# Two-relation graph layer: the low parts of the edge counts applied through a few selected rows

## The reference, cut to what matters

```python
w = jnp.einsum('rb,bio->rio', att, basis)
x_j = x[col]
for r in range(NUM_RELATIONS):
    gate = jax.nn.sigmoid(x_j @ gate_w[r, :, 0])
    msgs.append(gate[:, None] * x_j @ w[r])
msg = jnp.where((edge_type == 0)[:, None], msgs[0], msgs[1])
agg = jax.ops.segment_sum(msg, row, num_segments=x.shape[0])
return agg + x @ root + bias
```

## Time and profile before

| | |
|---|---|
| runs (three) | 842.68 us median, 841.76 to 845.55 |
| the profiled execution | 841.44 us, its span 839.4 us |
| TensorE (PE) busy | 811.3 us, 97% |
| TensorE weight loads (PEld) | 618.9 us, 74% |
| VectorE (DVE) | 555.1 us, 66% |
| ScalarE (ACT) | 397.6 us, 47% |
| GpSimd (POOL) | 279.4 us, 33% |
| DMA | 115.78 MB, 138 GB/s |

### The profile page before, as it was taken

The page is one execution under the profiler, slowest core; times in us unless marked ns, Lnnn a source line. Parts: engine busy times, 40 slices in busy tenths (PEclk is TensorE's granted clock), DMA queues, the critical chain, the costliest instruction groups (busy, mean ns, idle before and its releaser), DMA issues.

```text
span 839.4 us, 13163 instructions
## 1 busy us (share of the span) xinstructions
PE 811.3 (97%) x4174; PEld 618.9 (74%) x4175; DVE 555.1 (66%) x1223; ACT 397.6 (47%) x646; POOL 279.4 (33%) x296
## 2 busy tenths in 40 slices
PE   5999989999899999999999999999999999999998
PEld 3665646677578778778687787887777967688786
DVE  7999998787878677477656665683767666720210
ACT  5999985345455523366323465134562344530300
POOL 5000015434442235702366222556112725542200
PEclk9999999999999999999999999999999999999999
DMA  7899956727416544763473736547435786020100
GB/s 190 171 238 231 280 144 168 179 81 196 134 51 140 167 102 135 176 156 114 94 201 101 178 80 190 117 141 167 104 124 154 187 223 175 26 101 0 51 13 38
DMA packets 60655, 115.78 MB, mean 138 GB/s; under 512 B 4520, under 2 KB 5104, under 8 KB 60596
## 3 DMA queue, kind: packets, MB, share of 16 engines
q1 hardware_dynamic: 43412, 81.33, 40.2%
q10 hardware_dynamic: 17184, 33.69, 12.2%
HBM read 107.67 MB, written 7.34 MB: 137 GB/s over the span
## 4 chain that ended last, share of the span: by engine, by line
PE 67%; DVE 5%; ACT 1%; issue 1%; DVEq 0%
PE ring L2098 26%; PE ring L1788 19%; PE ring L2405 5%; PE ring L1806 5%; PE mix_ps L1817 4%; PE ring L2392 3%; PE ring L2333 1%; PE ring L2334 1%; DVE stats L1207 1%; PE ring L2287 1%; PE ring L2288 1%; PE ring L2292 1%; DVE xl L1585 1%; PE ring L2364 1%; DVE yp L1523 1%
## 5 line engine op out<-in xcount | busy, mean ns | idle before, releaser
L703 POOL TENSOR_TENSOR wl<-wraw,wh 128x512 fp32r<-128x512 f32 x140 | 181.1, 1324 | 265.2 <-ACT wh L809 253.7
L712 POOL TENSOR_TENSOR rstd<-ve,half 128x1 f32<-128x1 f32 x48 | 26.9, 561 | 209.0 <-DVE ve L1212 208.7
L1890 PE MATMUL ring<-ohs,ohd 128*128 128x512 f32 x312 | 80.0, 407 | 4.3 <-DVE ohs L1385 4.2
L1890 PEld LDWEIGHTS ring<-ohs,ohd 128*128 128x128 f32 x312 | 58.3, 193 | 30.1 <-issue 17.1
L1363 DVE SCALAR_TENSOR_TENSOR ohd<-iota,dstT,vals 128x256 fp32r x156 | 69.0, 477 | 3.4 <-issue 2.4
L809 ACT ACTIVATE wh<-wraw 128x2048 fp32r<-128x2048 f32 x35 | 66.8, 1909 | 5.2 <-PE ring L1788 4.9
L834 ACT ACTIVATE yT_h<-ring 128x512 fp32r<-128x512 f32 x32 | 18.4, 598 | 97.9 <-PE ring L1806 97.9
L858 ACT ACTIVATE ohs<-iota,minus_srcT 128x512 fp32r<-128x512 f32 x78 | 52.7, 714 | 8.7 <-issue 6.4
L1194 DVE TENSOR_TENSOR PT_l<-ring,PT_h 128x512 fp32r<-128x512 f32 x64 | 39.6, 681 | 16.0 <-ACT PT_h L834 16.0
L1817 PE MATMUL mix_ps<-quad,att_shift 120*32 120x512 f32 x384 | 46.8, 599 | 0.0
L834 ACT ACTIVATE qk_h<-ring,bias_columns 128x512 fp32r<-128x512 f32 x32 | 22.1, 690 | 51.8 <-PE ring L1788 43.7
(11 more groups left out here) (390 smaller groups left out, 2146.5 us busy)
## 6 DMA issues: line engine op xcount, KB each, us to landing
quad<-in_L_gnn_basis SPq DMA_DIRECT2D x60, 960.0 KB, 10.6
wraw<-in_L_gnn_m_w ACTq DMA_DIRECT2D x8, 1024.0 KB, 6.5
mix_scratch<-mixed SPq DMA_DIRECT2D x128, 32.0 KB
wraw<-in_L_gnn_wv ACTq DMA_DIRECT2D x4, 1024.0 KB, 8.1
wraw<-in_L_gnn_wq ACTq DMA_DIRECT2D x4, 1024.0 KB, 5.5
wraw<-in_L_gnn_wk ACTq DMA_DIRECT2D x4, 1024.0 KB, 5.3
wraw<-in_L_gnn_wo ACTq DMA_DIRECT2D x4, 1024.0 KB, 6.7
wraw<-mix_scratch ACTq DMA_DIRECT2D x4, 1024.0 KB, 5.7
```

What stands on the lines that cost most here:

```text
L703: last = g.tensor_tensor(wl[s][:, k, :], wraw[s][:, k, :], wh[s][:, k, :].bitcast(F32), ALU.subtract)
L1890: last = te.matmul(ring[:, banks[b], :], ohd[:, s, b, :], ohs[:, s, :], start=False, stop=False)
```

## The change

All of it is in the last stage.

- **Counts.** The matmuls with `C_l` are left out of `R(l, m)`: two matmuls for each relation and row tile in place of three. A count below 4096 has no low part, and among 16384 edges at most four counts can reach it, so at most four rows of each tile need one. VectorE finds in `far_flags` (after the first relation's four Z tiles) the largest count of each row, clears a selector `far_sel` of 8 x 128 columns and marks the rows at or above 4096. A product with a triangle of ones, the tile `order`, ranks them; `far_selectors` turns the ranks into selection columns. TensorE then gathers the chosen rows of `C_l` into a tile `far` (8 matmuls, once) and of `Z_h` into `near` (8 matmuls, for each l), both at full width, VectorE copies them to SBUF, and one matmul `near` by `far` goes into each `R(l, m)`. The gathering comes after `R(l, 0)`, and R(l, 0) and R(l, 1) are both closed after the matmuls of R(l, 1).
- **Gates.** `gwh` and `gwl` become one `gw` of four columns; 4 x two matmuls in place of 4 x three. The 4x512 result is copied by ScalarE as it is, four small fp32 products with a 4x2 matrix of ones and zeros (`gate_sum`) transpose it and add high and low parts, and ScalarE takes the exp of the 128x8 result.
- **Elsewhere.** GpSimd makes the triangle and the numbers between two weights' low parts; `far_sel`, `far` and `near` lie where `Cr` was; the small tables lie in `mask`, which is free by then. Three tiles are added to `n3` for l = 0 (`order`, `far`, `near`) and one for l = 1.

```diff
@@ tiles of the last stage @@
-                   + [n for l in range(2) for n in [("g", l)] + [("Z", l, r, t) for r in range(2) for t in range(4)]
-                      + [("R", l, t) for t in range(4)]], n2.end)
+                   + [("g", 0)] + [("Z", 0, 0, t) for t in range(4)] + [("Z", 0, 1, t) for t in range(3)]
+                   + ["order", ("Z", 0, 1, 3), "far", ("near", 0)] + [("R", 0, t) for t in range(4)]
+                   + [("g", 1)] + [("Z", 1, r, t) for r in range(2) for t in range(4)]
+                   + [("near", 1)] + [("R", 1, t) for t in range(4)], n2.end)
@@ GpSimd @@
+            low_weight(W3, slot(W3))
+            g.affine_select(out=far_upto, in_=ones[:], compare_op=ALU.is_ge, fill=0.0, base=0,
+                            pattern=[[1, P]], channel_multiplier=-1).then_inc(far_numbers, 1)
+            g.iota(far_no.rearrange("p (a e) -> p a e", e=STRIP), [[-FAR, 2 * NT], [1, STRIP]], base=1, channel_multiplier=0,
+                   allow_small_or_imprecise_dtypes=True).then_inc(far_numbers, 1)
+            low_weight(W3 + 1, slot(W3 + 1))
@@ ScalarE @@
-                a.activation(gate_e[:], ring[0:2, n3.bank(("g", l)), :], ACT.Exp, scale=-1.0).then_inc(gate_exp, 1)
+                a.activation(gate_raw, ring[0:4, n3.bank(("g", l)), :], ACT.Copy).then_inc(gate_raws, 1)
                 act.drain().then_inc(tile_taken, 1)
+                act.wait_ge(gate_rows, l + 1)
+                a.activation(gate[:], mix_ps[:, 0:2 * NT], ACT.Exp, scale=-1.0).then_inc(gate_exp, 1)
@@ VectorE @@
+            v.tensor_tensor(gate_sum, ident[0:4, 0:2], ident[0:4, 2:4], ALU.add).then_inc(gate_sums, 1)
...
+            def far_flags():
+
+                for r in range(2):
+                    v.reduce_max(far_top[:, r * NT:(r + 1) * NT], f(C_h[:, r, :, :]), AX.X).then_inc(far_step, 1)
+                v.memset(far_sel[:].bitcast(F32), 0.0).then_inc(far_step, 1)
+                dve.wait_ge(far_step, 3)
+                v.tensor_scalar(far_flag, far_top, EXACT, None, ALU.is_ge).then_inc(far_step, 1)
+
+            def far_selectors():
+                ready(n3, n3.base, "order")
+                dve.wait_ge(far_step, 4)
+                v.tensor_tensor(far_rank, bank(n3, "order")[:, 0:2 * NT], far_flag, ALU.mult).then_inc(tile_taken, 1)
+                taken(n3, n3.base, "order")
+                dve.wait_ge(far_numbers, 2)
+                each = lambda ap: ap.unsqueeze(2).broadcast_to([P, 2 * NT, STRIP])
+                v.tensor_tensor(far_eq.rearrange("p (a e) -> p a e", e=STRIP), far_no.rearrange("p (a e) -> p a e", e=STRIP),
+                                each(far_rank), ALU.is_equal).then_inc(far_step, 1)
+                dve.wait_ge(far_step, 5)
+                v.tensor_tensor(far_sel[:, :, 0:STRIP], far_eq.rearrange("p (a e) -> p a e", e=STRIP), each(far_flag), ALU.mult).then_inc(far_step, 1)
@@ VectorE, in the loop over l @@
+                        if l == 0 and r == 1 and t == 2:
+                            far_selectors()
+                    if l == 0 and r == 0:
+                        far_flags()
+                if l == 0:
+                    ready(n3, n3.base, "far")
+                    v.tensor_copy(far[:], bank(n3, "far")).then_inc(tile_taken, 1)
+                ready(n3, n3.base, ("near", l))
+                v.tensor_copy(near[:], bank(n3, ("near", l))).then_inc(tile_taken, 1)
@@ TensorE @@
+            def chosen_rows(name, of):
+
+                multiply(begin(n3, B, name), [(far_sel[:, r * NT + t, :], of[:, r, t, :]) for r in range(2) for t in range(NT)]
+                         ).then_inc(tile_ready, 1)
...
-                    for n, (lhs, rhs) in enumerate(three(gwh[:, l, k, :], gwl[:, l, k, :], h[:, k, :], hl[:, k, :])):
-                        last = te.matmul(out, lhs, rhs, start=k + n == 0, stop=k == KT - 1 and n == 2)
+                    te.matmul(out[0:4, :], gw[:, l, k, :], h[:, k, :], start=k == 0, stop=False)
+                    last = te.matmul(out[0:2, :], gw[:, l, k, 0:2], hl[:, k, :], start=False, stop=k == KT - 1)
...
+                        if l == 0 and r == 1 and t == 2:
+                            pe.wait_ge(far_numbers, 1)
+                            pe.wait_ge(far_step, 4)
+                            te.matmul(begin(n3, B, "order")[:, 0:2 * NT], far_upto, far_flag, start=True, stop=True).then_inc(tile_ready, 1)
                         if r == 0 and t == 2 - l:
-                            pe.wait_ge(gate_exp, l + 1)
+                            pe.wait_ge(gate_raws, l + 1)
+                            pe.wait_ge(gate_sums, 1)
                             pe.wait_ge(set_taken, SETS + 1)
                             for j in range(NT):
-                                last = te.transpose(mix_ps[:, 2 * j:2 * j + 2], gate_e[:, j * P:(j + 1) * P], ident[0:2, 0:2])
+                                last = te.matmul(mix_ps[:, 2 * j:2 * j + 2], gate_raw[:, j * P:(j + 1) * P], gate_sum, start=True, stop=True)
...
-                            if l == 0:
-                                pairs = three(z[:, m * P:(m + 1) * P], zl[:, m * P:(m + 1) * P], C_h[:, r, t, :], C_l[:, r, t, :])
-                            else:
-                                pairs = three(C_h[:, r, t, m * P:(m + 1) * P], C_l[:, r, t, m * P:(m + 1) * P], z, zl)
+                            for part in (z, zl):
+                                if l == 0:
+                                    te.matmul(out, part[:, m * P:(m + 1) * P], C_h[:, r, t, :], start=False, stop=False)
+                                else:
+                                    te.matmul(out, C_h[:, r, t, m * P:(m + 1) * P], part, start=False, stop=False)
+
+                def far_relations(m):
+                    c = slice(m * P, (m + 1) * P)
+                    lhs, rhs = (near[:, c], far[:]) if l == 0 else (far[:, c], near[:])
+                    te.matmul(outs[m], lhs, rhs, start=False, stop=True).then_inc(tile_ready, 1)
+
+                relations(0)
+                if l == 0:
+                    pe.wait_ge(far_step, 6)
+                    pe.wait_ge(c_ready, 2)
+                    chosen_rows("far", C_l)
+                chosen_rows(("near", l), Z_h)
+                relations(1)
+                taken(n3, B, ("near", l))
+                far_relations(0)
+                far_relations(1)
+                for m in range(2, NT):
+                    relations(m)
+                    far_relations(m)
```

More of the change, by code:

```diff
@@ L68 @@
 INTO_L3 = INTO_L2 + NT
+EXACT = 4096.0
+FAR = STRIP // (2 * NT)
+assert EDGES // EXACT <= FAR
 EPS = 1e-5
@@ L196, in program @@
         layer_bias = sb("layer_bias", [P, KT])
-        gate_e = mask[0:2, 0, :]
+        gate_raw = mask[0:4, 0, :]
+        gate_sum = mask[0:4, 2, 0:2]
+        far_upto = mask[:, 1, 0:P]
+        far_no = mask[:, 1, P:3 * P]
+        far_top = mask[:, 1, 3 * P:3 * P + 2 * NT]
+        far_flag = mask[:, 1, 3 * P + 2 * NT:3 * P + 4 * NT]
+        far_rank = mask[:, 1, 3 * P + 4 * NT:3 * P + 6 * NT]
+        far_eq = mask[:, 2, 2 * P:4 * P]
         gate = sb("gate", [P, 2 * NT])
@@ L331, in program @@
         C_l = sb("C_l", [P, 2, NT, NODES], F32R, ctx=c3)
-        Cr = [sb(f"Cr{r}", [P, NT, NODES], I16, ctx=c3) for r in range(2)]
+        counted = ExitStack()
+        Cr = [sb(f"Cr{r}", [P, NT, NODES], I16, ctx=counted) for r in range(2)]
+        counted.close()
+        far_sel = sb("far_sel", [P, 2 * NT, P], F32R, ctx=c3)
+        far = sb("far", [P, NODES], F32R, ctx=c3)
+        near = sb("near", [P, D], F32R, ctx=c3)
         c3.close()
@@ L402, in program @@
         row_bias_loaded = [sem(f"row_bias_loaded{j}") for j in range(2)]
+        gate_raws = sem("gate_raws")
         row_biased = sem("row_biased")
+        gate_sums = sem("gate_sums")
         end_bias_loaded = sem("end_bias_loaded")
@@ L413, in program @@
         c_ready = sem("c_ready")
+        far_numbers = sem("far_numbers")
+        far_step = sem("far_step")
         gate_exp = sem("gate_exp")
@@ L782, in _ @@
             block_lows(BLOCKS - 1, True)
-            for w in (W3, W3 + 1):
-                low_weight(w, slot(w))
+            low_weight(W3, slot(W3))
[4 more added lines that the diff above has]
+            low_weight(W3 + 1, slot(W3 + 1))
             for t in range(NT):
@@ L1291, in selectors @@
                 v.tensor_tensor(sel[:, 0, :], f(sel[:, 0, :]), f(sel[:, 1, :]), ALU.add)
-                v.tensor_copy(gwh[:], gates).then_inc(sel_step, 1)
+                v.tensor_copy(gw[:, :, :, 0:2], gates).then_inc(sel_step, 1)
                 v.tensor_copy(bg[:, :, 0:2], bias).then_inc(sel_step, 1)
@@ L1296, in selectors @@
                 dve.wait_ge(sel_step, 6)
-                v.tensor_tensor(gwl[:], gates, f(gwh[:]), ALU.subtract).then_inc(sel_step, 1)
+                v.tensor_tensor(gw[:, :, :, 2:4], gates, f(gw[:, :, :, 0:2]), ALU.subtract).then_inc(sel_step, 1)
```

(19 more changed lines are left out.)

9 lines of the change are left out of this document (4 added, 5 removed).

## The result

The changed kernel takes 836.43 us in the median of six runs (835.25 to 838.71), the kernel before, beside it on the same chip, 842.47 (six runs, 841.76 to 845.55). The ratio is 0.9923, with a 95% interval of 0.9909 to 0.9937: faster by 0.8%, 6.0 us by the medians. The forecast was 835.6 us, with a range of 833.2 to 838.6. The profiled execution took 836.25 us with a span of 834.4, where 834.3 and 832.3 were forecast.

The account below looks back on a forecast made before the run. TensorE bounds the kernel, busy 811.3 of 839.4 us. Terms -14.51 - 1.85 + 7.25 + 0.29 + 1.0 + 0.75 = -7.1 us give 835.6 us from the median of 842.68, range 833.2 to 838.6.

Parts of the forecast that it names:

- Removed matmuls, gatherings and closings: TensorE, last stage: 64 matmuls with `C_l` removed, -14.51 us; 32 gathering and closing matmuls of the same shape added, +7.25 us.
- The gate matmuls: Gates on TensorE: one matmul in three goes, 4 for each layer, 8 x 0.231 = 1.85 us saved.
- `order`: TensorE's ranking product in full fp32, 128 rows and 8 columns: 0.29 us added, nothing if it slips between two others.
- The small products: Gates: four fp32 products replace four transposes in each layer, 0.5 us more a layer, 1.0 for both (0.7 to 1.6).
- The stall before the second layer's products: TensorE waits 0.66 to 0.92 us, taken as 0.75, for ScalarE's gates' tile reading, held by the root weight's transfer.
- The wait for `hT_l`: Before the last gate matmuls: not new, ending 1.35 us after R(0, 3), covered by six matmuls of 1.39 us.
- The flags' cover: `far_flags` on VectorE is ready before TensorE reaches `order`: hidden, by 0.1 to 0.9 us.
- GpSimd, the copies, the banks: GpSimd's tables fit a 2.46 us gap, copies run under R(l, 1), shifted banks were taken earlier: no cost.
- The bounds: The main forecast's 834.5 to 836.8 us, from the products, the stall and spare time at `order`; chance 0.70.
- late flags: Rival, chance 0.12: VectorE's reductions or clearing are slower, TensorE waits 1 to 3 us at `order`, 836.6 to 838.6 us.
- the costly gathering: Rival, chance 0.05: selections and closings cost over 0.2267 us each, or closing hides a 2 to 3 us wait; 838.8 us.
- The fall of the clock: Rival, chance 0.03: a stall drops TensorE's clock from 2.4 to 1.2 GHz, each matmul losing 0.227 us; slower.

Follow-up runs that it names:

- the kernel with the transposes: Changed kernel, but TensorE transposes the gates' four rows as before and VectorE adds high and low parts: 834.48 us, ratio 0.9892.
- the kernel with the early reading: Changed kernel with gates transposed, VectorE adding the parts, and ScalarE reading the second layer's gates' tile before rounding the root weight: 833.93 us, ratio 0.9888.
- doubled flags: Changed kernel with VectorE computing the two row maxima of the counts twice, so the flags are late: 841.14 us, ratio 0.9973.
- changed again: The changed kernel as it is, measured and profiled once more against the kernel before: 835.9 us, ratio 0.9917.
- gates alone: The kernel before with only the gates' part of the change, the counts as before: 841.96 us, ratio 0.9993.
- later wait: Changed kernel with the row maxima computed twice and `order` moved behind the last Z tile: 837.79 us, ratio 0.9949.

## Why the prediction was right

The sum was -7.1 us and the stage became 7.20 us shorter. By its terms:

- **Removed matmuls, gatherings and closings** (-14.51 and +7.25): right. R of the first layer is 2.73 us shorter, and 12 x 0.2267 = 2.72 remain when 20 matmuls come in for 32. Behind the second layer's products it is 3.83 + 0.71 (the products' own) = 4.54, and 20 fewer are 4.53. The kernel without the gathering confirms 7.25 us by 7.38, of which 0.07 stand before the second layer's products and 0.07 are the products'.
- **The gate matmuls** (-1.85): right as work, 8 in 1.85 us where there were 12 in 2.77.
- **`order`** (+0.29): 0.12 us and 0.13 more for the tile behind it, 0.25.
- **The small products** (+1.0): mis-sized. They took 0.98 and 1.05 us for 0.34 each, +1.35, and the kernel with the transposes gives the same 1.3 back. I put them nearer to the transposes because only four rows are loaded; the larger products of the earlier trace rows, at 0.145 us an instruction, were the nearer end. The load of the stationary operand took 0.12 us for each of eight instructions (0.96 us), and the eight loads of 128 rows for the products of the earlier trace rows took 0.97. The Trainium skill, TensorE: Matmul & The Clock Gate, section LDWEIGHTS (loading the stationary operand), says that the load goes by the operand's columns and not by its rows; the trace agrees for these two. A transpose's load of the same four rows and 128 columns took 0.08 (0.32 us for four); why a product's load is longer, no run here shows. The Trainium skill, FP8 and Floating Point Precision, section TensorE Precision Notes, has true FP32 take four passes through the array. An estimate from that alone made the products of two columns next to free, and the 1.35 us speak against it.
- **The stall before the second layer's products** (+0.75): the mechanism exists, but its size was read from one landing of the transfer, and in the first profile it is all but absent. The products came 7.57 us after R(0, 3), not 7.95 to 8.21. TensorE's work is 7.29 us, so 0.28 us were lost, and 0.20 of that is the wait for `hT_l`: the kernel with the early reading, where ScalarE is not waited for, needs 7.50. At most 0.07 us is left for ScalarE. The idle time of 0.7 to 0.9 us that was to show the stall is not there. From the transfer's issue to the start of the rounding it took 4.95, 4.98 and 5.08 us in three executions with products (no gathering, doubled flags, changed), and they came after 7.50, 7.54 and 7.57; 5.41, 5.41 and 5.46 in three others (changed again, gates alone, later wait), with 7.88, 7.88 and 7.93. The upper end of 8.21 was a misreading: the 0.26 us between ScalarE's end and the weight load in the earlier trace rows were TensorE's own arrival, for where TensorE does wait, the load follows 0.05 us after ScalarE (785.74 to 785.79).
- **The wait for `hT_l`** (nothing, "not new"): it is new. Three matmuls for each value of k put nine ahead of that wait, two put six. `hT_l` was ready at 779.00 and the sixth matmul through at 779.03, as counted (1.35 us against 1.39), but the next weight load stands behind the same wait and began only at 779.05, and that cost 0.20 us.

The errors, +0.35 on the products and -0.47 on stall and wait together, nearly cancel. That the sum fits to 0.1 us is in that part luck. The conclusion drawn from them held all the same: the second layer's gates gave back all that they saved, 8.61 us from R(0, 3) to the end of the products against 8.55 before.

The terms put at nothing, and the bounds:

- **The flags' cover**: ready 0.8 us before TensorE, where 0.1 to 0.9 was argued for. Both reductions took 4.47 us, the clearing 0.91.
- **GpSimd, the copies, the banks** (nothing): as argued.
- **The bounds** 834.5 to 836.8 are wider than what is named for them: 0.3 us less to 0.6 more for the products, 0.09 less to 0.17 more for the stall and 0.29 less for `order` give 834.9 to 836.4.

The forecast of the span was 2.1 us low, though the stage was 0.1 us better than forecast. The step from one profiled span to the other passed over a spread that the profile of one execution can't show: the first 118 us differ by up to 1.7 us between executions of one kernel. The medians, 6.0 and 6.9 us apart in the two measurements, are less open to it.

Of the rivals, late flags and the costly gathering did not occur; the stall was all but gone in the first profile and there, at half its size, in the second. The fall of the clock did not occur in the stage either, but it is real: it came behind a wait of 3.5 us, and those of the change come to less than 0.6 us together in this part of the stage. Had the reductions run at half their rate, the case that I priced at 839 to 840 us, the run with four of them says 841 in the median, and 839 where the clock stayed up: I priced the wait there and not the clock behind it.

## What to carry to other kernels

Where one engine's chain has no gap, count its matmuls times their start-to-start time and look at each place where another engine hands over; the sum came within 0.1 us here, with two errors of 0.35 and 0.47 us that offset each other. A selection made by matmuls costs a full matmul for each tile that it reads at full width, however few rows it picks, and here that halved the saving. And removing work from the busy engine just ahead of a hand-over buys nothing until the other engine's chain is shortened as well: the gates' part of this change, in itself a third fewer matmuls, was worth 0.2 us, and 1.2 us more came from giving TensorE back its cheap transposes.

## What the hardware showed that was not expected

- A wait of 3.5 us on TensorE was followed by some 6 us at the granted clock 0.50 and cost 3.1 us on top of itself in the profiled execution; another of the ten shows a mean clock of 1.000. Idle times of 0.79 and 0.34 us cost no clock in the stage, while near 145 us the same idle time, 1.52 us in its longest piece, cost some 1.7 us in two executions and none in a third.
- A full fp32 product of a 4x128 stationary operand with two columns took 0.25 us (two instructions of 0.12), a transpose of the same rows 0.085.
- The same 1 MB transfer, issued by the same instruction, landed 4.95 to 5.46 us after its issue in twelve executions, and in the kernels with the small products that spread went through ScalarE into the end of the kernel.
- One and the same kernel reaches its 118th microsecond up to 1.7 us earlier or later.
